# An attention stage that transposes four blocks of X per pair instead of seven, and sums them afterwards

## The chip, the cores and the metric

One core of one Trainium2 chip runs the whole program. The metric is the device time of one execution in microseconds (us). Engines: PE (TensorE) multiplies and transposes, DVE (VectorE), ACT (ScalarE) and POOL (GpSimd) work elementwise, SP (SyncE) issues most transfers (DMAs). Each engine runs its own instructions in order, and semaphores order them among the engines.

## What is computed

The input x has 16 batches of 128 rows with 1024 columns, ctx 16 batches of 128 x 256. The reference is a cross attention and then a gated feed-forward network whose weights are unpacked from 4 bits:

```python
q, k, v = Wq @ xn, Wk @ ctx, Wv @ ctx            # xn = layernorm(x), per batch [128, 1024]
x = x + Wskip @ xn + softmax(q.T @ k / sqrt(128)) @ v
g, u = layernorm(x) @ Wg.T, layernorm(x) @ Wu.T  # 2752 features, weights dequantised
x = x + (silu(g) * u) @ Wd.T
```

## The kernel before, in words

**The feed-forward part** multiplies by Strassen's scheme in Winograd's form. X, the normalised rows of all batches, is seen as a 2 x 2 grid of blocks: the row half is one batch or the other of a pair of batches, the column half the even or the odd columns. Seven products need seven operands of X: X11, X21, X22 and the sums T1 = X12 - X11, T2 = X22 - T1, T3 = X22 - X12, T4 = X21 - T2. X12 itself is in no product. Each operand is held transposed in `xt`, as a 16-bit high half and a 16-bit low half (value minus high half). A feed-forward "instance" is seven products of 12 matmuls each (`product`, L560); instances 0 and 1 use the columns of pairs 0 to 3, and from instance 2 on those of pairs 4 to 7 are used too. Such an instance with its work on the other engines is called a tile.

**The attention** runs over 17 steps, `for i in range(STEPS)`. Step i does batch i, finishes batch i - 1, and prepares blocks of X for earlier pairs. A batch's 1024 columns are handled in two halves f. The order is written out by hand on every engine:

- PE: energies(i, 0); sums' blocks; values(i-1, 0); "between" blocks; energies(i, 1); probs_transposed(i-1, 1); "after" blocks; keys_values(i+1); values(i-1, 1); probs_transposed(i, 0). In a steady even step the blocks are T1, T2 and X11, in an odd one T3, T4, X21 and X22: seven for a pair of steps. Each is four transposes of 128 x 128 (`block_transposed`, L511).
- ACT: blocks' high halves (`block_hi`, L797), four exponentials per half (`exponentials`, L790), four scalings per half by the inverse totals (`normalize_probs`, L804), copies of the transposed probabilities (`probs_out`, L785), keys (L775) and values (L779). normalize_probs(i, 1) comes ahead of values_out(i+1) and probs_out(i, 0).
- DVE: negated maxima of the energies (`maxima`, L1224), blocks' low halves (`block_lo`, L1229), inverse totals (L1239), the residual sum (`add_attention`, L1235), row statistics (L1202, L1206) and normalising (L1216) before and after the attention, and in most steps a job that unpacks the first weights. The statistics of row i + 2 stand ahead of maxima(i, 1), the normalising of row i + 1 behind inverse_total(i, 1).
- POOL: inverse deviations (L364, L367), and the four sums of a pair from the normalised rows, in 32-bit (`blocks_of_x`, L380). They go to `mixed`, and the two normalised rows of a pair stand in `xn2`. PE then transposes X11, X21, X22 and the four sums.
- SP: loads ctx and x of batch i + 2 or later, stores rows, loads weights.

**PSUM.** Energies take banks 0 to 3, values bank 6. Everything else that PE transposes or multiplies for the attention goes through a ring of three banks in the order of `USES`; `bank_free` makes PE wait until the use three places earlier has been read out. For keys that is `s_vt_sb`, set by values_out; for a block `s_xt_lo`, set by DVE.

**Late blocks.** What the steps do not reach goes through one bank between the products of instances 0 and 1 (`LATE`, eight blocks), where a block waits until DVE has made the low half of the one before.

**Start and end.** SP loads ctx 0, then the whole first row (512 KB); ACT loads the four attention weights in one transfer. PE does ten warm-up matmuls. At the end each of 16 output rows is stored in one transfer after its last sum on DVE (L1762).

## Time and profile before

| | us |
|---|---|
| median of 3 runs (lowest, highest) | 1419.85 (1419.73, 1420.11) |
| the profiled execution | 1420.11 |
| its span, first to last instruction | 1418.3 |
| PE busy | 1398.0 (99%) |
| DVE, ACT, POOL busy | 1123.1, 683.1, 312.1 |
| steps of the attention, from the first energies to the first product | 8.8 to 223.1 |

The profiled execution is one of the three runs, 0.26 us above their median. Its span is 1.8 us shorter than its time. "Busy" is the time in which an engine has an instruction under way; matmuls are pipelined and their ends are modelled, so PE's pace is better read from the starts of groups in the timeline. In the timeline a row is start, duration, engine, line, operation, tiles, and in brackets the idle time before it with what ended it.

### The profile page before, as it was taken

Reading aid. Unit: us, or ns where it says so; the run is one execution under the profiler, and the core shown is the slowest. Engines: PE = TensorE matmul, PEld = TensorE weight load, DVE = VectorE, ACT = ScalarE, POOL = GpSimd, SP = SyncE. Lnnn points to the kernel's source line nnn. Section 1 sums busy time; section 2 is a strip of 40 time slices with the busy share of each in tenths; the row PEclk is TensorE's granted clock in tenths of the full one; section 3 lists DMA queues with packets and bytes.
Section 4 is the critical chain, followed back from the end, with each engine's and each line's share of the span. In section 5 each row is a group of like instructions: output and inputs, shape, how many; then the busy total and the mean of one; then the engine's idle time right before and its main releaser. Section 6 shows DMA issues by size and latency. Waiting matters only on the chain.

```text
span 1418.3 us, 19786 instructions
## 1 busy us (share of the span) xinstructions
PE 1398.0 (99%) x6510; PEld 690.6 (49%) x6510; DVE 1123.1 (79%) x1597; ACT 683.1 (48%) x1271; POOL 312.1 (22%) x365
## 2 busy tenths in 40 slices
PE   8999998999999999999999999999999999999998
PEld 6677764444444444444444444444444444444443
DVE  5898988878778788788787788788788788787476
ACT  5889894344444444444444444444444444434430
POOL 1243232022222212212222222212212212212200
PEclk9999999999999999999999999999999999999999
DMA  4322222176666666756856746747746747847796
GB/s 158 117 82 101 99 76 60 45 142 112 118 133 111 126 117 119 134 110 114 146 97 123 137 101 126 122 109 126 125 104 123 135 99 130 140 85 147 126 303 252
DMA packets 58551, 174.85 MB, mean 123 GB/s; under 512 B 7952, under 2 KB 10768, under 8 KB 54160
## 3 DMA queue, kind: packets, MB, share of 16 engines
q0 software_dynamic: 34560, 83.90, 38.2%
q1 hardware_dynamic: 23808, 90.20, 20.6%
q8 instruction: 20, 0.33, 0.1%
q10 hardware_dynamic: 144, 0.26, 0.1%
q14 instruction: 19, 0.16, 0.0%
HBM read 73.67 MB, written 100.66 MB: 123 GB/s over the span
## 4 chain that ended last, share of the span: by engine, by line
PE 90%; DVE 4%; ACT 3%; issue 2%; POOL 0%; POOLq 0%; DVEq 0%; ACTq 0%
PE ps L560 51%; PE ps L600 9%; PE ps L599 9%; PE ps L598 9%; PE ps L489 3%; PE ps L522 3%; PE ps L754 2%; PE ps L477 2%; PE ps L517 1%; PE ps L511 1%; ACT temps L790 1%; ACT temps L804 1%; PE ps L713 1%; DVE w_gu L1303 0%; PE ps L465 0%
## 5 line engine op out<-in xcount | busy, mean ns | idle before, releaser
L560 PE MATMUL ps<-xt,w_gu 128*128 128x512 f16 x3528 | 795.9, 379 | 2.7 <-DVE temps L1402 1.4
L560 PEld LDWEIGHTS ps<-xt,w_gu 128*128 128x128 f16 x3528 | 345.2, 98 | 417.9 <-DVE temps L1402 1.9
L916 ACT ACTIVATE stage<-ps,pow 128x512 f32<-128x512 f32 x300 | 204.2, 686 | 320.0 <-PE ps L600 318.3
L1442 DVE SCALAR_TENSOR_TENSOR stage<-ps,pow,stage 128x512 f32<-128x512 f32 x220 | 160.1, 747 | 101.0 <-ACT stage L916 63.3
L598 PE MATMUL ps<-park 128*128 128x512 f16 x560 | 212.2, 379 | 0.0
L599 PE MATMUL ps<-park 128*128 128x512 f16 x560 | 212.2, 379 | 0.0
L600 PE MATMUL ps<-park 128*128 128x512 f16 x560 | 212.2, 379 | 0.0
L405 POOL DMA_DIRECT2D out<-stage x80 | 70.5, 881 | 423.7 <-DVE stage L1442 423.7
L419 POOL DMA_DIRECT2D out<-stage x80 | 69.0, 863 | 297.4 <-ACT stage L916 297.4
L913 ACT CAST park<-temps 128x512 f16<-128x512 f32 x140 | 83.1, 614 | 64.9 <-DVE temps L1426 38.1
L1439 DVE TENSOR_TENSOR park<-temps,park 128x512 bf16<-128x512 f32 x140 | 98.3, 708 | 16.9 <-ACT park L913 13.9
L599 PEld LDWEIGHTS ps<-park 128*128 128x128 f16 x560 | 54.8, 98 | 66.1
L598 PEld LDWEIGHTS ps<-park 128*128 128x128 f16 x560 | 54.8, 98 | 66.1
L600 PEld LDWEIGHTS ps<-park 128*128 128x128 bf16 x560 | 54.8, 98 | 66.1
L412 POOL DMA_DIRECT2D out<-stage x60 | 66.8, 1113 | 6.7 <-DVE stage L1442 6.7
L489 PE MATMUL ps<-w_gu,park 128*128 128x256 f32 x256 | 62.8, 390 | 1.5 <-DVE park L1216 0.9
L790 ACT ACTIVATE temps<-ps,neg_max 128x256 f32<-128x256 f32 x128 | 59.3, 486 | 9.2 <-DVE neg_max L1224 9.2
L435 POOL TENSOR_TENSOR temps<-temps 128x512 f32<-128x512 f32 x20 | 30.7, 1533 | 150.1 <-DVE temps L1432 150.1
L522 PE MATMUL ps<-temps,w_gu 128*128 128x512 f32 x128 | 60.1, 592 | 0.0
L1303 DVE TENSOR_TENSOR w_gu<-raw,w_gu 128x1024 f16<-128x1024 f32 (+1 forms) x43 | 53.1, 1235 | 7.7 <-ACT w_gu L853 6.1
L804 ACT ACTIVATE temps<-temps,inv_total 128x256 f32<-128x256 f32 x128 | 54.7, 504 | 6.9 <-DVE inv_total L1239 6.9
L489 PEld LDWEIGHTS ps<-w_gu,park 128*128 128x128 f32 x256 | 48.0, 195 | 12.2 <-issue 5.3
(125 smaller groups left out, 1644.1 us busy)
## 6 DMA issues: line engine op xcount, KB each, us to landing
out<-stage POOLq DMA_DIRECT2D x80, 512.0 KB, 5.4
out<-stage POOLq DMA_DIRECT2D x140, 256.0 KB, 5.3
grid<-grids SPq DMA_DIRECT2D x136, 256.0 KB, 6.1
raw<-packed SPq DMA_DIRECT2D x34, 512.0 KB, 4.3
out<-stage SPq DMA_DIRECT2D x17, 512.0 KB, 2.6
stage<-x SPq DMA_DIRECT2D x13, 512.0 KB, 3.7
xt<-out SPq DMA_DIRECT2D x12, 512.0 KB, 11.5
out<-xt SPq DMA_DIRECT2D x12, 512.0 KB, 2.7
```

What stands on the lines that cost most here:

```text
L405: pool.dma_start(out[t, :, 0:NOUT], stage[:, d % 2, 0:NOUT], accum_op=ALU.add).then_inc(s_add11[d % 2], 16)
L489: mm = pe.matmul(ps_e[f][:, t, :], xn[b % XNS][:, cols], kk[:, par, :], start=True, stop=True)
L522: mm = pe.matmul(ps_o, v_t[:, par, h, :], prob_t[:, f, h, :], start=False, stop=(h == 1))
L560: mm = pe.matmul(bank, w_gu[e][:, wp, w, P * j:P * j + P], xt[:, xb, xp, j, cols], start=(fresh and n == 0), stop=(n == 3 * J - 1), skip_g ...
L598: pe.matmul(bank, h_hi[:, h, rows], w_d[:, 0, w, :], start=fresh, stop=False, skip_group_check=not fresh)
L599: pe.matmul(bank, h_hi[:, h, rows], w_d[:, 1, w, :], start=False, stop=False, skip_group_check=not fresh)
L600: return pe.matmul(bank, h_lo[:, h, rows], w_d[:, 0, w, :], start=False, stop=True, skip_group_check=not fresh)
L790: ex = act.activation(prob[:, NTH * f + t, :], ps_e[f][:, t, :], ACT.Exp, bias=neg_max[:, f, t:t + 1], accum_out=total[:, f, t:t + 1])
L913: act.copy(h_hi[:, block, :], src).then_inc(s_h_hi, 1)
L916: return act.activation(dst, ps[:, bank, :], ACT.Copy, scale=pow2[:, 10:11])
L1439: dve.tensor_tensor(h_lo[:, block, :], src, h_hi[:, block, :], ALU.subtract).then_inc(s_h_lo, 1)
L1442: return dve.scalar_tensor_tensor(out=part, in0=ps[:, bank, :], scalar=pow2[:, 10:11], in1=part, op0=ALU.mult, op1=ALU.add)
```

## The change

- PE transposes X11, X12, X21 and X22 of each pair and no sums. At most one block stands "between" and one "after" in a step: X21 of the pair before and X12 in an odd step, X22 and X11 in an even one. The "after" block now follows keys_values, and the "between" block precedes values(i-1, 0). Five blocks are late instead of eight.
- ACT copies X12 as a 32-bit block to `more` (here `x12`). DVE makes the four sums from the transposed blocks: one operand in PSUM, the other `x12` or an earlier sum. ACT makes their high halves (`sum_hi`), POOL the low halves (`sum_lo`, in place of `blocks_of_x`).
- `mixed` moves into columns of `xt` that only the last pair fills; that pair's sums go to rows 1 and 2 of `stage`. `xn2` has four rows instead of two.
- The order in a step: on ACT normalize_probs(i, 1) comes last, behind values_out and probs_out(i, 0). On DVE normalising row i + 1 and maxima(i, 1) come right behind add_attention(i-1, 0), and then the statistics of row i + 2.
- Start: row 0 is loaded first, in two halves with semaphores of their own; the attention weights come in two transfers. End: the last output row is stored in two halves.

```diff
+X12 = 7
-def blocks_of_step(i, which):
-    k = i // 2
-    found = {
-        "sums": [(k - 2, T3), (k - 2, T4)] if i % 2 else [(k - 2, T1), (k - 2, T2)],
-        "between": [(k - 1, X21)] if i % 2 else [],
-        "after": [(k - 1, X22)] if i % 2 else [(k - 1, X11)],
-    }[which]
+def block_of_step(i, which):
+    k = (i - 3) // 2
+    block = {"between": (k - 1, X21) if i % 2 else (k, X22), "after": (k, X12) if i % 2 else (k, X11)}[which]
+    return block if block[0] >= 0 else None
...
-LATE = [(6, T3), (6, T4), (7, X21), (7, X22), (7, T1), (7, T2), (7, T3), (7, T4)]
+XNS2 = 4
+LATE = [(LAST - 1, X21), (LAST, X12), (LAST, X22), (LAST, X11), (LAST, X21)]
+SUMS = [T3, T1, T2, T4]
...
+                if i == 0:
+                    for h in range(2):
+                        cols = slice(H * h, H * h + H)
+                        sp.dma_start(row(0)[:, cols], x[b, :, cols]).then_inc(s_first_x_in[h], 16)
                 sp.dma_start(ctx_sb[:, par, :], ctx_in[b, :, :]).then_inc(s_ctx_in[par], 16)
-                sp.dma_start(row(i), x[b, :, :]).then_inc(s_x_in[par], 16)
+                if i:
+                    sp.dma_start(row(i), x[b, :, :]).then_inc(s_x_in[par], 16)
...
-            for t in range(B):
+            for t in range(B - 1):
                 sp.wait_ge(s_last, 2 * t + 2)
                 sp.dma_start(out[t, :, :], acc(t)).then_inc(s_out, 16)
+            for oh in range(2):
+                o = slice(NOUT * oh, NOUT * oh + NOUT)
+                sp.wait_ge(s_last, 2 * (B - 1) + oh + 1)
+                sp.dma_start(out[B - 1, :, o], acc(B - 1)[:, o]).then_inc(s_out, 16)
...
-            def blocks_of_x(k, u):
-                pool.tensor_tensor(mixed[:, u - T1, :], a, b, ALU.subtract).then_inc(s_mixed, 1)
+            def sum_lo(k, u):
+                n = nth_sum(k, u)
+                pool.wait_ge(s_sum_hi, n + 1)
+                pool.tensor_tensor(xt_of(k, u, 1).rearrange("p j (h r) -> p j h r", h=2),
+                                   mixed(k, u).rearrange("p (j h) r -> p j h r", h=2),
+                                   xt_of(k, u, 0).rearrange("p j (h r) -> p j h r", h=2), ALU.subtract
+                                   ).then_inc(s_sum_lo, 1)
...
             for i in range(1, STEPS):
-                k = (i - 3) // 2 if i % 2 else -1
+                k = (i - 5) // 2
                 if k >= 0:
-                    blocks_of_x(k, T1)
-                    blocks_of_x(k, T2)
+                    sum_lo(k, T2 if i % 2 == 0 else T3)
                 if i + 2 < B:
                     inverse_deviation(0, i + 2)
-                if k >= 0:
-                    blocks_of_x(k, T3)
-                    blocks_of_x(k, T4)
+                if i % 2 and k >= 0:
+                    sum_lo(k, T1)
+                elif k >= 0:
+                    sum_lo(k, T4)
                 inverse_deviation(1, i - 1)
-            for u in (T1, T2, T3, T4):
-                blocks_of_x(B // 2 - 1, u)
+            for u in SUMS:
+                sum_lo(LAST - 1, u)
+            for u in SUMS:
+                sum_lo(LAST, u)
...
             for i in range(STEPS):
                 if i < B:
                     energies(i, 0)
-                for unit in blocks_of_step(i, "sums"):
-                    block_transposed(unit)
+                if block_of_step(i, "between"):
+                    block_transposed(block_of_step(i, "between"))
                 if i >= 1:
                     values(i - 1, 0)
-                for unit in blocks_of_step(i, "between"):
-                    block_transposed(unit)
                 if i < B:
                     energies(i, 1)
                 if i >= 1:
                     probs_transposed(i - 1, 1)
-                for unit in blocks_of_step(i, "after"):
-                    block_transposed(unit)
                 if i + 1 < B:
                     keys_values(i + 1)
+                if block_of_step(i, "after"):
+                    block_transposed(block_of_step(i, "after"))
...
-            act.dma_start(w_att, att_weights[:, :, :]).then_inc(s_weights_in, 16)
+            act.dma_start(w_att[:, 0:2, :], att_weights[:, 0:2, :]).then_inc(s_weights_in, 16)
+            act.dma_start(w_att[:, 2:4, :], att_weights[:, 2:4, :]).then_inc(s_more_weights_in, 16)
...
+                if u == X12:
+                    wait(act, s_mixed, nth_sum(k - 1, T1) + 1)
+                    act.copy(more[:, :], bank).then_inc(s_x12, 1)
...
-                if i < B:
-                    normalize_probs(i, 1)
+                if i % 2 == 0 and k >= 0:
+                    sum_hi(k, T3)
+                elif k >= 1:
+                    sum_hi(k - 1, T2)
                 if i + 1 < B:
                     values_out(i + 1)
                 if i < B:
                     probs_out(i, 0)
+                if i < B:
+                    normalize_probs(i, 1)
...
+            def sum_of_blocks(k, u):
...
+                a, b, op = {T3: (bank, x12, ALU.subtract), T1: (x12, bank, ALU.subtract),
+                            T2: (bank, mixed(k, T3), ALU.add), T4: (bank, mixed(k, T2), ALU.subtract)}[u]
+                dve.tensor_tensor(mixed(k, u), a, b, op).then_inc(s_mixed, 1)
+
+            def block_done(unit):
+                k, u = unit
+                for t in {X12: (), X22: (T3,), X11: (T1, T2), X21: (T4,)}[u]:
+                    sum_of_blocks(k, t)
+                if u != X12:
+                    block_lo(unit)
...
                 if i >= 1:
                     add_attention(i - 1, 0)
+                if 1 <= i and i + 1 < B:
+                    normalize(0, i + 1)
+                if 0 < i < B:
+                    maxima(i, 1)
+                if i == 0:
+                    maxima(0, 1)
                 if i + 2 < B:
-                    if i == 0:
-                        maxima(0, 1)
                     x_arrived(i + 2)
                     row_stats(0, i + 2)
-                for unit in blocks_of_step(i, "between"):
-                    block_lo(unit)
-                if 0 < i < B:
-                    maxima(i, 1)
...
                 if meanwhile:
                     meanwhile()
                 if i < B:
                     inverse_total(i, 1)
+                if block_of_step(i, "after"):
+                    block_done(block_of_step(i, "after"))
-                if 1 <= i and i + 1 < B:
-                    normalize(0, i + 1)
                 if i >= 1:
                     add_attention(i - 1, 1)
```

## Rows read from the trace of the kernel before

**Rows 1.** The page: busy us and share of the span of each engine.
```profile
PE 1398.0 (99%) x6510; PEld 690.6 (49%) x6510; DVE 1123.1 (79%) x1597; ACT 683.1 (48%) x1271; POOL 312.1 (22%) x365
```

**Rows 2.** Windows by stage: us, busy us (instructions) by engine, PEclk, DMA share.
```profile
32.01:57.66 25.65, 24.70 (x114) 17.14 (x113) 20.05 (x52) 21.25 (x66) 8.70 (x14) 1.00 0.52 153
57.66:214.76 157.10, 155.84 (x763) 112.27 (x763) 137.94 (x262) 139.46 (x405) 49.34 (x68) 1.00 0.26 89
214.76:223.08 8.32, 7.60 (x33) 4.38 (x33) 5.33 (x11) 4.23 (x9) 0.74 (x2) 1.00 0.16 63
223.08:273.86 50.78, 45.78 (x226) 22.37 (x224) 43.57 (x57) 16.88 (x25) 8.36 (x6) 1.00 0.25 63
```

**Rows 3.** Timeline of PE, steps 7 and 8: start, us, engine, line.
```profile
96.36 1.89 PE L489 MATMUL ps<-w_gu,park 128*128 128x256 f32 x8
...
101.54 0.63 PE L511 MATMUL ps<-ident,park 128*128 128x128 f32 x4
102.00 1.89 PE L489 MATMUL ps<-w_gu,park 128*128 128x256 f32 x8
103.73 1.04 PE L477 MATMUL ps<-ident,temps 128*128 128x128 f32 x8
104.61 0.70 PE L511 MATMUL ps<-ident,park 128*128 128x128 f32 x4
105.14 0.63 PE L465 MATMUL ps<-w_gu 128*128 128x256 f32 x2
...
109.56 1.97 PE L489 MATMUL ps<-w_gu,park 128*128 128x256 f32 x8
...
122.30 1.89 PE L489 MATMUL ps<-w_gu,park 128*128 128x256 f32 x8
```

**Rows 4.** Windows of single steps, 11 and 15.
```profile
148.30:162.50 14.20, 13.53 (x69) 9.59 (x67) 13.50 (x25) 11.70 (x35) 6.96 (x8) 1.00 0.24 85
202.43:214.76 12.33, 12.33 (x60) 8.78 (x61) 8.76 (x17) 11.48 (x35) 5.80 (x6) 1.00 0.24 86
```

**Rows 5.** Groups of instructions, 57.66 to 214.76, of ACT and DVE; last one whole run.
```profile
L790 ACT ACTIVATE temps<-ps,neg_max 128x256 f32<-128x256 f32 x96 | 44.6, 490 | 0.8 <-DVE neg_max L1224 0.8
...
L797 ACT CAST xt<-ps 128x512 f16<-128x512 f32 x42 | 23.6, 594 | 11.8 <-PE ps L511 11.8
...
L853 ACT CAST w_gu<-quant 128x1024 f16<-128x1024 f32 x1 | 1.1, 1054 | 0.0
...
L1229 DVE TENSOR_TENSOR xt<-ps,xt 128x512 f16<-128x512 f32 x42 | 27.5, 678 | 6.1 <-ACT xt L797 6.0
...
L913 ACT CAST park<-temps 128x512 f16<-128x512 f32 x140 | 83.1, 614 | 64.9 <-DVE temps L1426 38.1 <-DVE temps L1482 11.5 <-DVE temps L1476 9.1
```

**Rows 6.** Groups of instructions, 57.66 to 214.76, of POOL.
```profile
L380 POOL TENSOR_TENSOR park<-park 128x512 f32<-128x512 f32 x24 | 33.5, 1407 | 16.2 <-DVE park L1216 15.2 <-POOL park L380 1.0
```

**Rows 7.** Waits from 222 to 300 us: total, times, longest.
```profile
PE ps L511 <- DVE xt L1229: 3.7, 3, 1.7
```

**Rows 8.** Timeline of DVE after the attention.
```profile
227.27 0.68 DVE L1288 TENSOR_SCALAR quant<-raw 128x1024 int32<-128x1024 int32 x1
227.87 1.99 DVE L1289 TENSOR_SCALAR raw<-raw 128x1024 int32<-128x1024 int32 x1
```

**Rows 9.** Timeline of the start, DVE and PE.
```profile
11.84 1.22 DVE L1224 TENSOR_REDUCE neg_max<-ps 128x4 f32<-128x1024 f32 x1
...
17.03 1.97 PE L477 MATMUL ps<-ident,temps 128*128 128x128 f32 x8 [3.66 <-ACT temps L804]
18.79 3.62 PE L489 MATMUL ps<-w_gu,park 128*128 128x256 f32 x8
```

**Rows 10.** DMA issues from 1380 us on: KB each, us to landing.
```profile
out<-stage SPq DMA_DIRECT2D x4, 512.0 KB, 2.6
```

**Rows 11.** Window from 16 to 19 us.
```profile
16.00:19.00 3.00, 1.97 (x9) 1.98 (x10) 2.96 (x10) 3.00 (x12) 0.74 (x2) 0.50 0.19 74
```

**Rows 12.** Timeline of DVE, second maxima of step 7.
```profile
104.36 1.22 DVE L1224 TENSOR_REDUCE neg_max<-ps 128x4 f32<-128x1024 f32 x1
```

More of the change, by code:

```diff
@@ L1243, in step @@
                     maxima(i, 0)
-                for unit in blocks_of_step(i, "sums"):
-                    block_lo(unit)
+                if block_of_step(i, "between"):
+                    block_done(block_of_step(i, "between"))
                 if i >= 2:
```

161 lines of the change are left out of this document (93 added, 68 removed).

## The prediction, made before the changed kernel had run

> **What bounds the kernel now.** I read the page first: PE is busy for 99% of the span [rows 1]. That alone does not say that PE is the limit, because the ends of matmuls are modelled. So I took the windows by stage. The change works in the attention (8.8 to 223.1 us) and in the first two tiles of the feed-forward part, so those windows matter, with three engines side by side [rows 2]. In steps 4 to 15 (157.10 us) PE is busy for 155.84, ACT for 139.46 and DVE for 137.94. PE leads, with the two others at 88 to 89%. The proof that PE really sets the pace there is the timeline of PE over steps 7 and 8: each group of instructions starts where the one before has issued its last, a step with four blocks takes 13.20 us (96.36 to 109.56), one with three 12.74 (to 122.30), and the difference is the 0.46 us of one block's four transposes (101.54 to 102.00) [rows 3]. Without blocks a step is thus 11.36 us of PE work, and every block is paid for in full.
>
> Waits appear in three places: steps 2 and 3 (25.65 us for three blocks, where PE's work is 24.1), some later steps (step 11, in which DVE has the first weights' low halves to make, takes 14.20 [rows 4]), and the first tile after the attention.
>
> **Part 1: 24 blocks less on PE.** Each of the 8 pairs transposes 4 blocks instead of 7. Of the 24 removed, 18 lie in steps 4 to 15 (42 become 24), two in steps 2 and 3 (three become one), one in step 16 (three become two) and three in the late blocks (eight become five). At 0.46 us the whole is worth 11.0 us, 8.3 of them in steps 4 to 15. PE's floor there becomes 11 x 12.28 + 11.41 = 146.5 us: two blocks in each step, and step 15 without keys, 12.33 us now with four blocks [rows 4]. Against 157.1 that is up to 10.6 us, since 2.3 us of the present time is waiting.
>
> **Part 2: what takes its place.** DVE makes four sums per pair from PSUM instead of four low halves: it had seven block instructions per pair (678 ns each [rows 5]) and has seven. ACT had seven copies and has eight: three high halves and X12 out of PSUM (594 ns), four high halves of sums out of SBUF. The nearest row for those is the cast of h, SBUF to SBUF in the same shape, 614 ns [rows 5]. One more copy per pair is 0.5 to 0.6 us, 3.0 over six pairs. So ACT needs 142.5 us of PE's 146.5. Now ACT idles for 17.6 us of 157.1, of which 11.8 is waiting for a block's transposes [rows 5]. If all of that goes and the other 5.8 us stay (they are round trips to DVE for the maxima and the inverse totals), steps 4 to 15 take 142.5 + 5.8 = 148.3 us. If none goes they take 160.1. These are my two ends.
>
> Where between? The new order takes much of this waiting out. The row statistics no longer stand between the energies and the second maxima. The transposed first probabilities go out before the second are normalised, so values(b, 0) wait for less. The weight jobs on DVE (up to some 2.5 us) now end well before the second normalisation is due. Against it: after X11 DVE has three instructions in a row (two sums and the low half, 1.8 us), then the attention's sum and the row statistics, before the next step's maxima. Laid out with the row durations, this ends 0.2 us late in a plain even step and up to 1.7 us late in one with the longest job. I take 0.45 us per pair, 2.7 in all. The two sets of weight casts on ACT, after steps 9 and 13 (two instructions each, 1.1 us for one of 128x1024 [rows 5]), had the slack of a slower step to hide in; now they have almost none, and I charge 1.5 us each, 3.0. That gives 146.5 + 5.7 = 152.2, a gain of **4.9** (bounds 8.8 and -3.0).
>
> **Part 3: steps 2, 3 and 16.** Steps 2 and 3 take 25.65 us; PE's work after is 2 x 11.36 + 0.46 = 23.2. They are held by the chain energies, maxima, exponentials, probabilities, which the new order shortens by the row statistics' 1.4 us before the second maxima. I take 23.85, a gain of **1.8** (0.3 to 2.4). Step 16 takes 8.32 us, with one block less and a wait of 0.7 that the second of its sums causes: **1.2** (0.5 to 1.6).
>
> **Part 4: POOL.** Its four subtractions per pair (1407 ns [rows 6]) become four others of the same shape with a 16-bit operand and result; I take the same price (between nothing and half as much again). POOL is busy for 49 of 157 us, which hides either. What queues behind them are the two inverse deviations; their normalisations stand half a step later on DVE, so 1.4 us is covered. If that cover went, each would delay DVE by up to 1.4 us.
>
> **Part 5: the first two tiles.** PE waits 3.7 us here for DVE's low halves [rows 7], since one bank serves all late blocks. The first tile keeps four late blocks, the second has one of four: three fewer are worth 1.4. X22 no longer waits for DVE but for ACT's copy of X12. But DVE is what PE waits for in the first tile, and it gets seven block instructions there instead of four, 1.8 us more, and POOL now does eight subtractions in this stretch instead of four. Beside POOL a DVE instruction over SBUF takes 1.99 us where its twin takes 0.68 [rows 8]: 1.3 us lost on one instruction. I take a gain of **0.5** (-2 to +3). The Trainium skill (GPSIMD Engine Reference, Key points) says that GpSimd contends only with VectorE instructions in a two-port mode or with two inputs from SBUF. By that rule the new sums, which read a PSUM bank, are free of it in the loop, and only the weight jobs of this stretch suffer; if the four further subtractions cost them what that one did, twice over, this term would be -2, not 0.5. The trace does not speak against it: the low halves, which read PSUM, have a mean of 678 ns though some run beside POOL [rows 5].
>
> **Part 6: the two ends.** Row 0 of x is now loaded first and in halves. DVE's first maxima start at 11.84 us, and what sets that time is DVE's two rounds of statistics and normalising before them; PE then waits 3.66 us for the first probabilities [rows 9]. The first half is issued 0.4 us earlier and is half as long. SP's queue issues one transfer more, so ctx 0, ctx 1 and row 1 start 0.45 us later, and ACT's queue one more, before it has work; ctx 0 must then land by 6.7, when the keys start, and row 1 by 7.2. Statistics start about 1.4 us earlier; the first energies are held by the keys' chain behind the warm-up and gain only 0.4. DVE can then take the maxima near 10.4: **1.3** (0 to 1.5). At the end the last store of 512 KB (2.6 us to landing [rows 10]) is split, so that 256 KB follow the last sum: **0.4** (0 to 0.7). By the Trainium skill (DMA: Bandwidth & Descriptors, Anatomy of one DMA) about 2 us of a transfer are fixed whatever its size, so by that page the halves could save at most 0.6 here.
>
> **Sum.** 4.9 + 1.8 + 1.2 + 0.5 + 1.3 + 0.4 = 10.1 us. The profiled execution took 1420.11 us (span 1418.3), 0.26 above the median: 1420.1 - 10.1 = **1410.0 us**.
>
> **The rivals.**
> *A. The chain, not PE, sets the step.* For it: steps 2 and 3 have few blocks and take 12.8 us each all the same, against 12.95 for a mean step now [rows 2, 3]. If blocks removed only turn into waits, steps 4 to 15 gain nothing, steps 2 and 3 0.3, step 16 0.7: 0.3 + 0.7 + 0.5 + 1.3 + 0.4 = 3.2, or 1416.9 us. Against it: the order that caused those waits is the very thing changed. Chance 0.13.
> *B. The waits go.* ACT at its lower end (8.8), then 2.2, 1.5, 2.5 in the tiles, 1.3 and 0.5: 16.8, or 1403.3 us. One mechanism could add to it: the granted clock stands at 0.50 from about 16 to 23 us, after PE had idled since 13.4 [rows 9, 11]. If the shorter chain ends that idle time before the clock falls, the transposes and first energies of step 1 run at the full level; the group of energies that takes 3.62 us there takes 1.89 in step 7, and some 2 us would be saved: 1401.3. The Trainium skill (TensorE: Matmul & The Clock Gate, Why this matters for your kernels) has the same cause, a gap of idle time between bursts; the gap here shrinks by about 1 us only, so I don't count on it. Chance 0.14.
> *C. A new wait for a bank, and slower.* The ring has three banks, and the second of the two probability groups at a step's end now takes the bank of keys(i+1), free only after ACT's values_out. Between the end of energies(i, 1) and that group PE has 0.88 + 0.46 + 3.98 = 5.3 us of work [rows 3]. ACT and DVE have in that time: maxima 1.2, exponentials 1.9 (44.6 us over 24 groups [rows 5]), a block 0.5, keys 0.4, a sum 0.5, values 0.3: 4.8. The maxima start 0.63 us after the energies' last issue today (103.73 to 104.36 [rows 3, 12]), so nothing is to spare, and every delay of DVE beyond that goes straight into PE's time. If the sums ahead of it made it 1.3 us later in each of 13 steps, 17 us would be lost against the 12.8 gained without the 0.45 per pair: 1420.1 - 12.8 + 17 = 1424.3 us. It turns slower from 1.0 us per step. Against it: 1.4 us of statistics leave exactly this place, and 0.7 of normalising and 0.6 of a second block instruction come. Chance 0.05.
>
> **Numbers.** Forecast 0.68, A 0.13, B 0.14, C 0.05. About 0.2% (2.8 us) is what a measurement of this kernel can tell from no change. Of A, whose gain is 3.2, I count 0.03 as within it. So faster 0.68 + 0.14 + 0.10 = 0.92, same 0.03, slower 0.05. The forecast's own bounds give about 1404 to 1415; the range reaches into B and A: 1402.5 to 1416.5.
>
> **What would show it.** Right: a pair of steps near 25.0 us in PE's timeline, with groups still butted together in plain steps, and ACT above 93% busy. Wrong in part 2: long idle time of ACT before a block's copy, or of PE before the second probability group. Part 5: waits of PE at the late blocks in the first tile still near 3.7 us in sum. Part 6: the first maxima near 10.4 us. A clock at 1.00 from 13 to 25 us is B's mark. A step of 13 us or more throughout would prove the forecast wrong.

## The result and the profile after

| | before, us | after, us |
|---|---|---|
| median (lowest, highest), 4 runs each | 1419.83 (1419.73, 1420.11) | 1409.67 (1408.32, 1411.42) |
| the profiled execution | 1420.11 | 1408.32 |
| its span | 1418.3 | 1406.3 |

The ratio is 0.9927, with a 95% interval of 0.9915 to 0.9940: 10.2 us faster by the medians, against 10.1 predicted. The profiled execution of the changed kernel is the fastest of its four, so the two traces differ by 11.8 us.

The page, with the busy time of each engine:

```profile
PE 1386.1 (99%) x6414; PEld 678.3 (48%) x6414; DVE 1118.0 (79%) x1597; ACT 689.6 (49%) x1279; POOL 310.3 (22%) x365
```

Against [rows 1] PE has 96 instructions less (24 blocks of four transposes) and 11.9 us less work; ACT has eight instructions and 6.5 us more.

The windows by stage: length, then busy us (instructions) of PE, PEld, DVE, ACT and POOL, then PEclk and the DMA share. The first four are steps 2 and 3, steps 4 to 15, step 16, and the first 17 products, among which all late blocks stand (in both kernels the stretch ends where the 18th product starts); the last two lie at the start:

```profile
28.59:52.27 23.68, 23.41 (x107) 16.15 (x105) 18.76 (x51) 20.34 (x62) 3.73 (x10) 1.00 0.56 165
52.27:202.87 150.60, 148.22 (x692) 103.95 (x691) 132.30 (x260) 143.55 (x409) 47.69 (x66) 1.00 0.27 92
202.87:211.93 9.06, 7.55 (x29) 4.14 (x29) 6.34 (x13) 6.02 (x13) 3.04 (x4) 1.00 0.15 60
211.93:265.09 53.16, 47.38 (x225) 22.27 (x224) 47.22 (x63) 21.27 (x33) 12.23 (x11) 1.00 0.23 60
16.00:19.00 3.00, 2.57 (x16) 2.39 (x17) 2.96 (x9) 3.00 (x12) 0.74 (x2) 1.00 0.36 138
19.00:22.00 3.00, 3.00 (x10) 1.51 (x9) 1.86 (x4) 2.91 (x9) 0.00 (x0) 1.00 0.00 0
```

In steps 4 to 15 PE is busy for 148.22 of 150.60 us and ACT for 143.55, 95%, where it had 89% [rows 2]. The stage is 6.5 us shorter. PE's timeline over step 8 shows how close it runs to its floor; this is the view of [rows 3]:

```profile
101.92 1.89 PE L521 MATMUL ps<-w_gu,park 128*128 128x256 f32 x8
103.65 0.63 PE L538 MATMUL ps<-ident,park 128*128 128x128 f32 x4
104.11 1.02 PE L544 MATMUL ps<-park,w_gu 128*128 128x512 f32 x2
104.97 1.88 PE L549 MATMUL ps<-temps,w_gu 128*128 128x512 f32 x4
106.69 1.89 PE L521 MATMUL ps<-w_gu,park 128*128 128x256 f32 x8
108.42 1.04 PE L509 MATMUL ps<-ident,temps 128*128 128x128 f32 x8
...
110.17 0.63 PE L538 MATMUL ps<-ident,park 128*128 128x128 f32 x4
110.64 1.02 PE L544 MATMUL ps<-park,w_gu 128*128 128x512 f32 x2
111.50 1.88 PE L549 MATMUL ps<-temps,w_gu 128*128 128x512 f32 x4
113.22 1.28 PE L509 MATMUL ps<-ident,temps 128*128 128x128 f32 x8
114.33 0.60 PE L521 MATMUL ps<-w_gu,park 128*128 128x256 f32 x2
```

The step takes 12.41 us (101.92 to 114.33), a pair some 24.8, and each group starts where the one before has issued its last, but for one place: the second probability group takes 1.28 us where the first takes 1.04. The 0.24 us between them is a wait for the bank that rival C named. The waits of PE and of its weight loads over steps 4 to 15 (total us, times, longest):

```profile
PE ps L538 <- ACT temps L814: 2.1, 2, 1.3
...
PEld ps L509 <- ACT w_gu L808: 2.9, 11, 0.3
```

L808 is values_out: 11 waits of up to 0.3 us. The two waits at a block (L538) are those behind the weight casts after steps 9 and 13.

Where the 11.8 us between the two executions come from, by the starts of groups:

| stretch | before | after | gained |
|---|---|---|---|
| to the first energies of step 1 | 18.79 | 17.36 | 1.43 |
| step 1 | 13.22 | 11.23 | 1.99 |
| steps 2 and 3 | 25.65 | 23.68 | 1.97 |
| steps 4 to 15 | 157.10 | 150.60 | 6.50 |
| step 16 | 8.32 | 9.06 | -0.74 |
| the first 17 products, late blocks among them | 54.92 | 53.16 | 1.76 |
| from there to DVE's last sum | 1136.50 | 1138.00 | -1.50 |
| DVE's last sum to the end of the span | 3.8 | 3.2 | 0.6 |

Together 12.0, the difference of the spans (1418.3 and 1406.3); the execution lies 2.0 us above its span where it lay 1.8 above, which makes 11.8.

### The profile page after: what moved, and what is told of

It is laid out like the page before. It is cut to its first block, busy times and chain, and to the rows that moved or that the text cites. A ratio compares the mean times of both kernels' runs of the same rounds, so it can differ in the third digit from the quotient of the medians.

```text
span 1406.3 us, 19596 instructions
## 1 busy us (share of the span) xinstructions
PE 1386.1 (99%) x6414; PEld 678.3 (48%) x6414; DVE 1118.0 (79%) x1597; ACT 689.6 (49%) x1279; POOL 310.3 (22%) x365
## 4 chain that ended last, share of the span: by engine, by line
PE 92%; DVE 3%; ACT 3%; issue 1%; DMA 0%; POOL 0%; SPq 0%; DVEq 0%; POOLq 0%; ACTq 0%
PE ps L586 52%; PE ps L624 9%; PE ps L625 9%; PE ps L626 9%; PE ps L549 3%; PE ps L521 3%; PE ps L782 2%; PE ps L509 2%; PE ps L741 1%; PE ps L544 1%; ACT temps L845 1%; ACT temps L819 1%; PE ps L538 1%; DVE neg_max L1272 0%; DVE park L1263 0%
## 5 line engine op out<-in xcount | busy, mean ns | idle before, releaser
L958 ACT ACTIVATE stage<-ps,pow 128x512 f32<-128x512 f32 x300 | 204.4, 687 | 321.3 <-PE ps L626 315.9
L521 PE MATMUL ps<-w_gu,park 128*128 128x256 f32 x256 | 60.5, 380 | 0.5 <-ACT w_gu L804 0.5
L549 PE MATMUL ps<-temps,w_gu 128*128 128x512 f32 x128 | 60.1, 592 | 0.0
L521 PEld LDWEIGHTS ps<-w_gu,park 128*128 128x128 f32 x256 | 47.4, 190 | 12.8 <-issue 7.2
## 6 DMA issues: line engine op xcount, KB each, us to landing
xt<-out SPq DMA_DIRECT2D x12, 512.0 KB, 11.9
```

The costliest lines, as they stand in the source:

```text
L521: mm = pe.matmul(ps_e[f][:, t, :], xn[b % XNS][:, cols], kk[:, par, :], start=True, stop=True)
L549: mm = pe.matmul(ps_o, v_t[:, par, h, :], prob_t[:, f, h, :], start=False, stop=(h == 1))
L958: return act.activation(dst, ps[:, bank, :], ACT.Copy, scale=pow2[:, 10:11])
```

## The experiments

Every ratio is against the kernel before, timed on the same chip. What is said to be slower or faster than the changed kernel goes by its median of 1409.67 us, from the set of runs above.

| run | median (lowest, highest) | ratio, 95% interval |
|---|---|---|
| before_fewer_transposes | 1416.13 (1415.89, 1416.38) | 0.9973 (0.9962, 0.9983) |
| before_new_order | 1420.17 (1418.25, 1421.13) | 1.0002 (0.9992, 1.0012) |
| after_old_act_order | 1424.61 (1423.71, 1426.02) | 1.0032 (1.0021, 1.0043) |
| after_old_dve_order | 1420.78 (1419.08, 1422.41) | 1.0006 (0.9996, 1.0015) |
| after_double_blocks | 1420.44 (1418.42, 1422.69) | 1.0003 (0.9994, 1.0013) |
| after_values_first | 1410.38 (1409.56, 1410.64) | 0.9930 (0.9913, 0.9947) |
| after_split_casts | 1409.15 (1408.21, 1409.79) | 0.9924 (0.9908, 0.9941) |
| after_late_order | 1408.64 (1406.79, 1409.96) | 0.9918 (0.9902, 0.9935) |
| after_old_ends | 1411.91 (1410.84, 1412.98) | 0.9944 (0.9929, 0.9959) |
| after_filler | 1409.36 (1407.71, 1410.24) | 0.9925 (0.9911, 0.9938) |
| before_filler | 1421.45 (1419.76, 1421.99) | 1.0008 (0.9998, 1.0017) |
| best | 1406.98 (1406.50, 1408.33) | 0.9911 (0.9894, 0.9927) |

### Less work for PE in the old order

```diff
-                for j in range(J):
+                for j in range(1 if u >= T1 and unit not in LATE else J):
```

> The kernel before, but the sums' blocks inside the steps (26 of them) have one of their four transposes instead of four, so their values in X's operands are left wrong. PE is relieved of 26 x 0.75 x 0.46 = 9.0 us; the orders of ACT and DVE stay the old ones. Theory (PE sets the pace, the order matters little): most of it comes back, 7 to 9 us faster, 1411 to 1413. Rival A (the old order's chain takes over once PE has less to do): under 4 us faster, above 1416, with the steps staying near 12.8 us.

3.7 us faster, where PE lost 9.0 us of work. The waits of PE over the steps from 52 to 202 us in this kernel:

```profile
PE ps L511 <- DVE xt L1229: 2.1, 6, 0.5
PE ps L465 <- ACT temps L785: 1.6, 2, 1.0
PE ps L477 <- DVE xt L1229: 1.0, 2, 0.7
```

A pair of steps now takes 25.21 us (94.83 to 120.04) where it took 25.94: 0.73 of the 1.38 us taken away in a pair. The rest stands as waits. Steps 4 to 15 take 153.66 us, 3.4 less than before, for 8.3 us of work taken away there. In the old order the chain over ACT and DVE is the limit just under PE's own, as rival A had it.

### The new order with the old work

The kernel before, with its seven blocks and its sums, but normalize_probs(i, 1) last on ACT and normalising and maxima(i, 1) ahead of the statistics on DVE:

```diff
-                if i < B:
-                    normalize_probs(i, 1)
                 if i + 1 < B:
                     values_out(i + 1)
                 if i < B:
                     probs_out(i, 0)
+                if i < B:
+                    normalize_probs(i, 1)
...
                 if i >= 1:
                     add_attention(i - 1, 0)
+                for unit in blocks_of_step(i, "between"):
+                    block_lo(unit)
+                if 1 <= i and i + 1 < B:
+                    normalize(0, i + 1)
+                if 0 < i < B:
+                    maxima(i, 1)
+                if i == 0:
+                    maxima(0, 1)
                 if i + 2 < B:
-                    if i == 0:
-                        maxima(0, 1)
                     x_arrived(i + 2)
                     row_stats(0, i + 2)
-                for unit in blocks_of_step(i, "between"):
-                    block_lo(unit)
-                if 0 < i < B:
-                    maxima(i, 1)
...
-                if 1 <= i and i + 1 < B:
-                    normalize(0, i + 1)
```

> The kernel before with all its seven blocks, and only the new order of ACT (the second normalisation last) and DVE (normalising and the second maxima ahead of the row statistics). Theory (PE sets the pace in steps 4 to 15, whose waits are 2.3 us): 1 to 4 us faster, from steps 2, 3, 11 and 14. Rival (the order is the larger part of the gain): 5 us or more faster.

The order alone brings nothing (1.0002), neither the 1 to 4 us of my theory nor the 5 of its rival. The trace shows why the sum is nothing: step 2 begins 1.05 us earlier (30.96 for 32.01), but steps 4 to 15 take 159.28 us, 2.2 more than before, and the first product starts at 223.08 in both. With seven blocks a pair the new order makes waits of its own; PE's waits from 28 to 222 us in this kernel:

```profile
PE ps L465 <- ACT temps L785: 2.2, 3, 1.2
PE ps L477 <- DVE xt L1229: 1.8, 5, 0.8
```

where the kernel before has 0.3 and 0.6 us for these two. So the two halves of the change do not add up. In steps 4 to 15 less work alone gains 3.4 us, the order alone loses 2.2, and the change, which has both (and PE's own new order), gains 6.5.

### The old orders with the new work

On ACT:

```diff
+                if i < B:
+                    normalize_probs(i, 1)
                 if i % 2 == 0 and k >= 0:
                     sum_hi(k, T3)
...
                 if i < B:
                     probs_out(i, 0)
-                if i < B:
-                    normalize_probs(i, 1)
```

> The changed kernel with the second normalisation back in its old place on ACT, ahead of the sum's high half, the values and the first probabilities. Theory: these three come 1.6 us later, and the second probability group and values(i, 0) then wait; the ring's slack was already used up, so 0.5 to 1.5 us per step, 6 to 15 us slower than the changed kernel. Rival (there is slack on ACT): within 2 us of the changed kernel.

On DVE, with ACT as in the change:

```diff
-                if 1 <= i and i + 1 < B:
-                    normalize(0, i + 1)
-                if 0 < i < B:
-                    maxima(i, 1)
                 if i == 0:
                     maxima(0, 1)
                 if i + 2 < B:
                     x_arrived(i + 2)
                     row_stats(0, i + 2)
+                if 0 < i < B:
+                    maxima(i, 1)
...
                 if block_of_step(i, "after"):
                     block_done(block_of_step(i, "after"))
+                if 1 <= i and i + 1 < B:
+                    normalize(0, i + 1)
```

> The changed kernel with DVE's old order: row statistics ahead of the second maxima, normalising row i + 1 after the inverse total. The second maxima come 0.7 us later. Theory: the wait of the second probability group for its bank grows from 0.24 us by 0.5 to 0.7 per step, 5 to 10 us slower than the changed kernel. Rival: ACT has slack before the exponentials, within 2 us.

With the old order on ACT the kernel is slower than the one before, by 0.32%, and 15 us slower than the change. PE's waits from 52 to 202 us in that kernel:

```profile
PE ps L509 <- ACT w_gu L808: 15.3, 11, 1.9
```

and with the old order on DVE:

```profile
PE ps L521 <- issue: 4.8, 5, 1.0
PE ps L509 <- ACT w_gu L808: 3.1, 9, 0.6
```

The first is rival C's mechanism at full size: the second probability group needs the bank of keys(i+1), values_out frees it, and behind four scalings and a sum's cast it does so some 1.4 us late in each step (11 waits). The second costs all of the gain too, 11 us, more than the 5 to 10 I expected, and I had named only one of its causes. The bank wait grew; but the largest wait is that of the first energies (L521), for which the profile names no releaser. DVE's timeline shows what it is. A row of DVE and one of PE, where step 9 begins:

```profile
119.42 0.80 DVE L1263 TENSOR_SCALAR park<-w_gu,mv,rstd 128x1024 f32<-128x1024 f32 x1
...
120.32 1.97 PE L521 MATMUL ps<-w_gu,park 128*128 128x256 f32 x8 [0.96 <-issue]
```

L1263 normalises row i + 1, which the next step's energies read; last but one in DVE's step, behind two sums and a low half, it ends 0.1 us before they start. Where both orders are new they are two conditions of one gain, not two gains.

### Does PE set the new pace?

Each in-loop block's four transposes are issued twice, into the same bank:

```diff
-                for j in range(J):
+                for j in list(range(J)) * (1 if unit in LATE else 2):
```

> The changed kernel with every block inside the steps transposed twice into the same bank: 27 x 0.44 = 11.9 us more of PE work, nothing else changed. Theory (PE sets the pace even now): 10 to 12 us slower than the changed kernel. Rival (ACT or DVE sets it now): less than 7 us, since waits absorb the rest.

10.8 us slower for 11.9 us of added work. The steps tell it without the scatter of the times: a plain step takes 13.39 us for 12.41, 0.97 more for two blocks, the two steps with casts 0.47 more, steps 4 to 15 together 10.5 more for 24 blocks. At the casts the wait of 2.1 us became 1.1, since slower steps give ACT slack; PE's waits from 52 to 202 us in this kernel:

```profile
PE ps L538 <- ACT temps L814: 1.1, 2, 0.8
```

In the changed kernel added work of PE is paid in full, except where the casts stand. That it would also be given back in full, were it taken away, this run does not show.

### The two waits that are left in the loop

The bank wait of 0.24 us per step: values_out goes ahead of the sum's cast.

```diff
+                if i + 1 < B:
+                    values_out(i + 1)
                 if i % 2 == 0 and k >= 0:
                     sum_hi(k, T3)
                 elif k >= 1:
                     sum_hi(k - 1, T2)
-                if i + 1 < B:
-                    values_out(i + 1)
```

> The changed kernel with the values' copy ahead of the sum's high half on ACT. Theory: the wait of 0.24 us before the second probability group in odd steps is for the bank that this copy frees; it goes, and steps 4 to 15 become 1 to 2 us shorter. Rival (the wait moves to the probabilities' copy or to POOL's low half): under 0.5 us.

Nothing gained: steps still take 12.41 us. My theory fell. The row of ACT in the changed kernel had said so already; values_out itself waits, for PE's values (L549), and asking earlier only makes it wait longer (0.63 us in this run):

```profile
113.42 0.37 ACT L808 COPY w_gu<-ps 128x256 f32<-128x256 f32 x1 [0.16 <-PE ps L549]
```

The program says what for: the attention's values stand in two buffers, and values_out(i + 1) writes the one that values(i - 1, 1) reads. So the copy can't end before PE has finished that group, and the probability group right behind it waits whatever ACT's order is. A third buffer was not tried.

The casts: the two instructions of each set on ACT go to two steps, and the last low half on DVE to step 15.

```diff
                 if i == 9:
-                    plain_hi(0, 0)
+                    act.wait_ge(s_weight, 1)
+                    act.copy(w_hi(0, W11, 1), q[:, 0:512]).then_inc(s_weight_hi, 1)
+                elif i == 10:
+                    act.wait_ge(s_weight, 2)
+                    act.copy(w_hi(0, W12, 2), r).then_inc(s_weight_hi, 1)
                 elif i == 13:
                     mixed_hi(0, 0, 0)
+                elif i == 14:
                     mixed_hi(0, 0, 1)
...
-                14: lambda: mixed_lo(0, 0),
+                14: lambda: mixed_lo(0, 0, 0),
+                15: lambda: mixed_lo(0, 0, 1),
```

> The changed kernel with the weights' casts on ACT spread over four steps (one each after steps 9, 10, 13 and 14) and the last low half on DVE in step 15. Theory: PE's waits of 1.1 us in step 10 and 1.5 us in step 14 shrink to some 0.3 each: 1.5 to 2.5 us faster. Rival: each cast costs its whole 1.1 us wherever it stands, since ACT has no slack: under 0.7 us.

PE's waits from 52 to 202 us in this kernel:

```profile
PE ps L538 <- ACT temps L814: 0.6, 2, 0.3
```

1.5 of 2.1 us of waiting are gone, and from the first energies of step 10 to the second of step 15 it takes 68.08 us for 69.43, 1.35 less. The median moved by 0.5 only, less than the scatter of either kernel, so the gain is shown in the trace and not by the times.

### Step 16 and the first tile

In step 16 ACT copies the block X22 before it scales the last probabilities, DVE takes the attention's sum ahead of normalising, and in the tile the late block precedes the weights' nibbles:

```diff
                     block_hi(block_of_step(i, "between"))
+                if i == B:
+                    normalize_probs(B - 1, 1)
...
-                if i < B:
+                if i < B - 1:
                     normalize_probs(i, 1)
...
+                if i == B:
+                    add_attention(i - 1, 0)
                 if i >= 2:
                     normalize(1, i - 2)
...
-                if i >= 1:
+                if 1 <= i < B:
                     add_attention(i - 1, 0)
...
+                    block_done(LATE[0])
                     job_nibbles(1)
-                    block_done(LATE[0])
```

> The changed kernel with three moves at the end of the attention: DVE finishes the first late block before it unpacks the second job's nibbles; in step 16 DVE adds the attention before it normalises, and ACT copies the block X22 before it scales the last probabilities. Theory: PE's waits of 2.79 us in the first tile and of 0.72 and 0.78 us in step 16 become under 1 us together: 2 to 3.5 us faster. Rival (the same DVE work then ends later in the first tile, and PE waits there instead): under 1 us.

From the second energies of step 15 to the first product it takes 14.14 us, not 15.75: 1.6 gained. The first 17 products gave 0.6 back (53.78 for 53.16): PE's wait of 2.79 us at a late block fell to 0.64, but a product then waited 1.17 for DVE and the next late block 1.82. DVE is busy without a gap from 220 to 225 us there; its order decides only who waits. The median is 1.0 lower, under the 2 to 3.5 that I expected.

### The start, the end and the clock

The old ends: row 0 whole and behind ctx 0, the four attention weights in one transfer, the last output row in one (the waits that go with them are left out here).

```diff
-                if i == 0:
-                    for h in range(2):
-                        cols = slice(H * h, H * h + H)
-                        sp.dma_start(row(0)[:, cols], x[b, :, cols]).then_inc(s_first_x_in[h], 16)
                 sp.dma_start(ctx_sb[:, par, :], ctx_in[b, :, :]).then_inc(s_ctx_in[par], 16)
+                if i == 0:
+                    sp.dma_start(row(0), x[b, :, :]).then_inc(s_first_x_in[0], 16)
...
-            act.dma_start(w_att[:, 0:2, :], att_weights[:, 0:2, :]).then_inc(s_weights_in, 16)
-            act.dma_start(w_att[:, 2:4, :], att_weights[:, 2:4, :]).then_inc(s_more_weights_in, 16)
+            act.dma_start(w_att, att_weights[:, :, :]).then_inc(s_weights_in, 16)
...
-            for t in range(B - 1):
+            for t in range(B):
                 sp.wait_ge(s_last, 2 * t + 2)
                 sp.dma_start(out[t, :, :], acc(t)).then_inc(s_out, 16)
-            for oh in range(2):
...
-                sp.dma_start(out[B - 1, :, o], acc(B - 1)[:, o]).then_inc(s_out, 16)
```

> The changed kernel with the old start (ctx 0 first, row 0 in one transfer, one transfer of the attention weights) and the old last store. Theory: the first maxima go back towards 11.8 us, the idle stretch of PE before the first probabilities is long enough again for the clock to fall in every execution, and the end is 0.6 us later: 2.5 to 4 us slower than the profiled execution of the changed kernel, 1 to 3 above its median. Rival (the two ends are worth under 1 us together): within 1 us of the median.

2.2 us slower by the medians, within the 1 to 3 that I expected. Filler: PE gets idle-time matmuls into the unused values bank ahead of the first probability group (10 in the changed kernel, 13 in the one before):

```diff
                 if i < B:
+                    if i == 0:
+                        for _ in range(FILL):
+                            pe.matmul(ps_o[:, 0:P], ident[:, :], ident[:, :], start=True, stop=True)
                     probs_transposed(i, 0)
```

> The changed kernel with ten more warm-up products of the identity in PE's idle stretch before the first probabilities are transposed. Theory: the scatter of the changed kernel (1408.3 to 1411.4) is the clock, which falls in some executions after that idle stretch and in others not; with the stretch filled it never falls, and all executions lie within 0.5 us of 1408.3. Rival (the scatter comes from transfers, or from the wait of 1.3 us seen late in the trace): the scatter stays.

> The kernel before with thirteen such products in the same place. Theory: the clock no longer falls from 16 to 23 us and 1.5 to 2 us are saved, 1418 or below. Rival (the chain through the first probabilities sets step 1 anyway): under 0.7 us.

The start of step 1 in PE's timeline, three kernels. The changed one with the old ends (PE's clock fell to half at 17.6 us):

```profile
16.96 1.43 PE L503 MATMUL ps<-ident,temps 128*128 128x128 f32 x8 [3.47 <-ACT temps L837]
18.19 3.28 PE L515 MATMUL ps<-w_gu,park 128*128 128x256 f32 x8
```

the changed one, in its own profiled execution:

```profile
16.43 1.09 PE L509 MATMUL ps<-ident,temps 128*128 128x128 f32 x8 [2.63 <-ACT temps L845]
```

and the one before, with filler:

```profile
17.92 1.89 PE L490 MATMUL ps<-w_gu,park 128*128 128x256 f32 x8
...
22.92 1.89 PE L523 MATMUL ps<-temps,w_gu 128*128 128x512 f32 x3 [2.25 <-ACT temps L789]
```

With filler in the kernel before, the energies run at the full clock (1.89 us for the 3.62 of [rows 9]), and nothing is gained: PE then waits 2.25 us for the probabilities of step 0, whose chain over ACT and DVE sets the time of step 1 in the old order, and the clock falls at 24.0 us instead, where it stretches the values and the second energies (22.92 to 25.46 to 28.13) with no wait left to hide it. Step 2 begins at 33.33 us, 1.3 later than without filler, and the median is 1.6 higher, which the interval (0.9998 to 1.0017) leaves at the edge of noise. The rival (the chain sets step 1) was right in kind. In the changed kernel the filler kept the start at the full clock, but the clock fell at 221.8 us, behind the wait in the first tile, and the median moved by 0.3 only. The five executions lie between 1407.71 and 1410.24 us, so the scatter that the filler was to end is still there. The row of the window from 222.1 to 225.1 us of that run, in the columns of the windows above:

```profile
222.10:225.10 3.00, 3.00 (x9) 1.08 (x8) 3.00 (x4) 1.55 (x2) 1.20 (x1) 0.50 0.00 0
```

### All that helped, together

Filler, the late order, the split casts, and values_out first (which had brought nothing, and was left in).

> All of these together: filler products at the start, the values' copy first, the late order and the spread casts. If the parts add up: 4.5 to 7 us faster than the changed kernel's best execution, 1401.5 to 1404. If they share one bound (ACT's queue), 1405 to 1407.

1406.98 us, at the upper end of the 1405 to 1407 that I had given for parts that share a bound, and not the 1401.5 to 1404 of parts that add up; that ACT's queue is this bound was not tested. It is 0.9911 of the kernel before, and 2.7 us under the median of the change, whose fastest run (1408.32) lies at this one's slowest (1408.33). The intervals of the two ratios overlap, and they are from different sets of runs; so it beats the kernel before surely, the change by the medians alone. PE's waits at the late blocks are 0.64 and 1.81, and the windows of the start and of the first tile stand at the full clock:

```profile
16.00:19.00 3.00, 2.45 (x16) 2.28 (x17) 2.96 (x9) 3.00 (x13) 0.74 (x2) 1.00 0.07 26
...
222.10:225.10 3.00, 1.94 (x9) 0.69 (x7) 3.00 (x4) 1.19 (x2) 1.32 (x1) 1.00 0.00 0
```

## Why the prediction was right, and which of its terms were not

**Parts 1 and 2, steps 4 to 15: right in kind, 1.6 too low, and one term right by luck.** Predicted 4.9, measured 6.5 (the bounds were 8.8 and -3.0). PE sets the pace there, and ACT, at 95%, did not become the bound. The terms of the 152.2 us come out as follows. PE's floor of 146.5 was 1.2 too high: the groups of step 8 without the bank wait add up to 12.17 us, not 12.28, since the 11.36 us read from [rows 3] had 0.1 us of short waits in it (104.61 to 105.14 is 0.53 us for four transposes, where others take 0.46). The casts were to cost 3.0 and cost 2.6 (step 10 takes 13.49 and step 14 13.92 for 12.41). "0.45 us per pair" of DVE lateness, 2.7 in all, did not come: PE waits for DVE nowhere in these steps. In its place stands the bank wait, 0.24 us in each of 11 steps, 2.6 in all, which was in no term; rival C had counted ACT and DVE on the way to that bank, and not that the copy waits for PE's own values. That the two are of one size is chance. The two groups of ACT and DVE over steps 4 to 15 that answer to [rows 5], and POOL's to [rows 6]:

```profile
L838 ACT CAST xt<-xt 128x512 f16<-128x512 f32 x23 | 14.7, 639 | 0.0
L832 ACT CAST xt<-ps 128x512 f16<-128x512 f32 x18 | 10.7, 592 | 0.0
...
L1278 DVE TENSOR_TENSOR xt<-ps,xt 128x512 f16<-128x512 f32 x18 | 12.3, 681 | 0.0
...
L1297 DVE TENSOR_TENSOR xt<-ps,xt 128x512 f32<-128x512 f32 x12 | 8.2, 683 | 0.0
...
L405 POOL TENSOR_TENSOR xt<-xt 128x512 f16<-128x512 f32 x22 | 25.5, 1160 | 1.9 <-ACT xt L838 1.9
```

ACT's 11.8 us of waiting for blocks [rows 5] are gone, as the upper bound wanted; the sum's cast cost 639 ns (614 assumed), DVE's sums 683 ns, the same as a low half (681).

**The argument had a gap.** "Every block is paid for in full" was read from a timeline without waits [rows 3]. That shows what PE does at the present pace, not how far below it the chain of the other engines lies. The run with fewer transposes in the old order shows how near it was: less than half of PE's 9.0 us came back. The prediction was saved because it priced the new order together with the removed work and took most of the waits as gone, which nothing in its rows proved.

**Part 3: steps 2 and 3 right, step 16 with the wrong sign.** 23.68 us against 23.85. For step 16 I had a gain of 1.2, "one block less and a wait of 0.7 that the second of its sums causes"; it lost 0.74. I looked at PE's queue alone. Rows of the changed kernel in step 16, of PE, ACT and DVE:

```profile
207.76 0.71 PE L538 MATMUL ps<-ident,park 128*128 128x128 f32 x4 [0.72 <-DVE xt L1278]
209.25 1.12 PE L544 MATMUL ps<-park,w_gu 128*128 128x512 f32 x2 [0.78 <-DVE stage L1310]
...
204.06 1.75 ACT L845 ACTIVATE temps<-temps,inv_total 128x256 f32<-128x256 f32 x4
205.67 0.62 ACT L832 CAST xt<-ps 128x512 f16<-128x512 f32 x1
...
206.32 0.69 DVE L1297 TENSOR_TENSOR xt<-ps,more 128x512 f32<-128x512 f32 x1 [1.71 <-ACT xt L832]
```

normalize_probs(15, 1), now last in step 15, stands on ACT ahead of X22's copy; DVE waits 1.71 us for that copy with the attention's sum queued behind, and PE waits twice. The scalings have only changed the queue that they delay: from the end of one step to the start of the next. In the loop a whole group of energies covers that, in step 16 there are none. The late order gained 1.6 us there.

**Part 4: right, and cheaper.** POOL's instruction takes 1160 ns, not 1407; nothing hangs on it.

**Part 5: 1.8, not 0.5, within the bounds.** The waits at the late blocks are 3.2 us (predicted: still near 3.7):

```profile
220.54 0.72 PE L538 MATMUL ps<-ident,park 128*128 128x128 f32 x4 [2.79 <-DVE xt L1278]
...
227.30 0.72 PE L538 MATMUL ps<-ident,park 128*128 128x128 f32 x4 [0.40 <-DVE xt L1278]
```

Three blocks less are 1.4 of it, and 0.5 of waiting went too. DVE's seven block instructions did not make the wait longer; I take this to be because fewer late blocks meet at one bank, which no run shows. DVE instructions do get slower beside POOL: DVE's normalising and nibbles, both over SBUF, take 1.64 us beside POOL's subtractions, where the same lines take 0.81 and 0.64 to 0.69 elsewhere:

```profile
215.39 1.64 DVE L1263 TENSOR_SCALAR park<-stage,mv,rstd 128x1024 f32<-128x1024 f32 x1 [1.00 <-POOL rstd L399]
216.95 1.64 DVE L1358 TENSOR_SCALAR quant<-raw 128x1024 int32<-128x1024 int32 x1
...
215.32 2.72 POOL L405 TENSOR_TENSOR xt<-xt 128x512 f16<-128x512 f32 x2
```

The Trainium skill (GPSIMD Engine Reference, Key points) names VectorE instructions in a 2-port mode or with two SBUF inputs as those that contend with GpSimd. The trace agrees as far as it goes: these two took twice as long and more, and the sums, with one operand in PSUM, kept their 683 ns through the loop; which mode the two were in it does not say. The -2 that I had worked out from it did not come.

**Part 6: the start half of what was said, and made up by the clock.** The first maxima came at 11.23 us, not 10.4, 0.6 earlier than before and not 1.4; DVE's timeline shows why:

```profile
4.01 0.69 DVE L1249 BATCH_NORM_STATS2 stats<-stage 128x6 f32<-128x512 f32 x1 [3.13 <-DMA stage<-x]
5.28 0.69 DVE L1249 BATCH_NORM_STATS2 stats<-stage 128x6 f32<-128x512 f32 x1 [0.58 <-DMA stage<-x]
```

DVE could start on the second half of the row only 1.27 us after the first, and so half of the lead was lost. PE's wait fell from 3.66 to 2.63 us, and its transposes of step 0's probabilities start at 16.43 us for 17.03. That is 0.60 us. Step 1 began 1.43 us earlier all the same, near the 1.3 predicted, but the other 0.83 is the clock: the group takes 0.93 us to its successor, not 1.76 as at half clock. The agreement is luck. The end gave 0.6 (0.4 predicted). A half of 256 KB lands in 2.1 us here, where the whole row of 512 KB takes 2.6 [rows 10]. The 2 us that the prediction took from the Trainium skill (DMA: Bandwidth & Descriptors, Anatomy of one DMA) are stated there for transfers that GpSimd issues, and these are SP's; the bound of 0.6 held all the same. The run with the old ends is 2.2 us slower; its trace has lost the clock at the start too, so these are the ends and some of the clock.

**B's extra, the clock.** In the profiled execution it came: 1.00 in both windows of the start, where it was 0.50 ([rows 11] has the first). I had not counted on it because the idle time shrinks by only 1 us. What it is worth can be read from a trace of the same order that lost it: with the late order, which differs from the change only behind step 15, step 2 begins at 30.01 us, not 28.59. So the clock is 1.4 of the 3.4 us that were gained up to there (32.01 to 28.59). Another 1 us comes with the order on ACT and DVE: in the kernel before with that order alone step 2 begins at 30.96 us, though the clock was at half there for 3.4 us and not for 6.8, so that order and clock are not quite apart. Of the 1.99 us that step 1 gained, then, not all is the clock; five kernels with the new order and a lost clock take 12.6 to 12.9 us for that step, where the kernel before takes 13.22.

**What was not in the sum.** From the 18th product to the last sum the changed kernel takes 1.5 us more. 1.3 of it is one wait:

```profile
1329.12 0.39 PE L624 MATMUL ps<-park 128*128 128x512 f16 x1 [1.31 <-ACT stage L958]
```

It stands in the traces of all nine variants of the changed kernel (0.9 to 1.3 us) and in none of the kernel before and its three, the one with the new order among them. PE waits for a copy of ACT (L958) that itself comes after 3.73 us of idle time, for which the profile names no releaser. Why a change in the attention brings it some 1100 us later was not tried, and stays open.

That the total is right to 0.1 us is therefore luck: in the two traces the forecast had 1.6 too little in the loop, 1.3 in the tiles and 2.0 in step 1, against 1.9 too much in step 16 and 1.5 given back later, and the profiled execution is 1.4 us under the median.

## What to carry to other kernels

A timeline without waits proves who leads, not by how much: before counting removed work as time, ask how far below lies the next chain, and whether an experiment that removes only the work would show it. Work removed and an order that shortens the chain were worth 3.4 and -2.2 us alone in steps 4 to 15, and 6.5 together. And where an instruction is moved to the end of an engine's step, follow it into the next step, and above all into the last one, where the work that covered it is missing.

## What the runs showed of the hardware

- **The clock falls in some executions, not in others, after the same wait.** PE waits 2.79 us at a late block of the first tile in five traces (the change, filler, old ends, values first, split casts); the clock stayed at 1.00 in the change and fell to 0.50 in the other four. At the start it stayed at 1.00 after a wait of 2.63 us in the change and even of 3.66 in the split casts, and fell after 2.75 with the late order, where the window from 16 to 19 us has 0.65, and after 3.66 in the kernel before. So the length of the wait alone did not decide it here. The cost can be read: 1.4 us at the start (above), and 1.0 us in the first tile, where the run with filler takes 45.02 us from the third product to the 18th and the change 44.00. The other three runs of the change had a mean clock of 0.998 to 0.999 and took 1.3 to 3.1 us longer. That the clock is most of its scatter is likely, not shown. The Trainium skill (TensorE: Matmul & The Clock Gate, Why this matters for your kernels) names idle gaps between bursts as the cause; each fall here stands at such a gap, but not each such gap has a fall.
- **POOL took 1160 ns for a subtraction of 128x512 with a 16-bit operand and result,** and 1407 with all three in 32 bits [rows 6]. The old ones also read every other column of one or two operands, so the type is not the only difference.
- **Two halves of a row, issued one behind the other, did not land together:** DVE could start on the second half 1.27 us after the first, more than the 0.69 us that its work on the first took.
